# In the second attention, the softmax probabilities are multiplied by the inverse totals on GpSimd instead of VectorE

## What is computed

```
q = einsum('btd,ndh->btnh', x, q_kernel)             # 16 query heads of 128
k, v = einsum('bsd,ckdh->cbskh', x, kv_kernel)       # 8 key and value heads
q, k = rms_norm(q, q_scale), rms_norm(k, k_scale)
q, k = apply_rope(q, positions), apply_rope(k, positions)
mask = (j <= i) & (i - j < 128)
logits = einsum('btkgh,bskh->bkgts', q * 0.0884, k), masked
probs = softmax(logits, axis=-1)
enc = einsum('bkgts,bskh->btkgh', probs, v)
out = einsum('btnh,nhd->btd', enc, out_kernel)
```

## Time and profile before

| | us |
|---|---|
| median of 3 runs | 989.39 |
| lowest, highest | 989.05, 1001.19 |
| the profiled execution | 989.41 |
| its span | 987.8 |
| tiles 0 to 7 of attention b, in the span | about 403.7 to 713 |
| DVE busy in the span | 630.9 (64%) |
| POOL busy in the span | 431.9 (44%) |
| PE busy in the span | 779.2 (79%) |

### The profile page before, as it was taken

One profiled execution on the slowest core, in us unless ns is written; L12 is line 12 of the kernel. 1 busy time (PEld: TensorE's weight loads), 2 busy tenths in 40 slices (PEclk: granted clock), 3 DMA queues, 4 the chain that ended last, 5 costly groups with the idle time before them and its releaser, 6 DMA issues.

```text
span 987.8 us, 17657 instructions
## 1 busy us (share of the span) xinstructions
PE 779.2 (79%) x4548; PEld 663.9 (67%) x4548; DVE 630.9 (64%) x2152; ACT 505.6 (51%) x1274; POOL 431.9 (44%) x340
## 2 busy tenths in 40 slices
PE   5897837989898306789999999999878689988841
PEld 4465726888788204567887878788766688888830
DVE  3565624667667267689778788797465467776522
ACT  2332314667677322565565665556423477777621
POOL 2004773657666513123122132130647267667551
PEclk9997977999999659799999999999959799999955
DMA  9955736888798430000000000000234689889645
GB/s 351 426 208 198 259 125 187 210 203 224 195 228 186 91 107 1 1 1 1 1 1 1 2 1 1 1 17 1 107 118 142 196 217 229 215 217 227 147 90 167
DMA packets 65591, 130.85 MB, mean 132 GB/s; under 512 B 8388, under 2 KB 36420, under 8 KB 63872
## 3 DMA queue, kind: packets, MB, share of 16 engines
q1 hardware_dynamic: 41104, 93.77, 28.5%
q0 software_dynamic: 24432, 36.44, 17.6%
HBM read 75.25 MB, written 54.92 MB: 132 GB/s over the span
## 4 chain that ended last, share of the span: by engine, by line
PE 34%; DVE 18%; issue 15%; DMA 15%; POOL 8%; ACT 6%; SPq 1%; DVEq 1%; POOLq 1%; ACTq 1%
DMA raw<-in_w_gate_up 6%; PE bank L315 6%; POOL token_rows L1791 6%; PE bank L317 5%; PE bank L316 5%; DMA over<-token_rows 3%; PE bank L852 3%; PE bank L817 3%; DVE over L1670 2%; PE bank L841 2%; PE bank L650 2%; DVE halves L1498 2%; DVE over L1626 2%; DVE over L1632 2%; PE bank L558 2%
## 5 line engine op out<-in xcount | busy, mean ns | idle before, releaser
L315 PE MATMUL bank<-halves 88*128 88x256 f32 (+2 forms) x548 | 193.4, 353 | 32.0 <-DVE halves L1498 19.0
L317 PE MATMUL bank<-halves 88*128 88x256 f32 (+2 forms) x548 | 173.5, 317 | 0.0
L316 PE MATMUL bank<-halves 88*128 88x256 f32 (+2 forms) x548 | 173.3, 316 | 0.0
L315 PEld LDWEIGHTS bank<-halves 128*128 128x128 f32 (+1 forms) x548 | 108.8, 198 | 51.7 <-issue 41.1
L1791 POOL DMA_INDIRECT token_rows<-xn,slot_ids x96 | 98.8, 1030 | 101.8 <-issue 69.3
L316 PEld LDWEIGHTS bank<-halves 128*128 128x128 f32 (+1 forms) x548 | 109.9, 201 | 0.9
L317 PEld LDWEIGHTS bank<-halves 128*128 128x128 f32 (+1 forms) x548 | 108.6, 198 | 1.0
L1480 DVE TENSOR_TENSOR over<-over,bank 128x176 f32<-128x176 f32 x128 | 42.6, 333 | 72.8 <-ACT over L1026 72.3
L1893 POOL TENSOR_TENSOR over<-over 128x512 f32<-128x512 f32 x16 | 20.6, 1285 | 144.5 <-DVE over L1632 144.5
L1165 ACT ACTIVATE over<-over,nb,rqs 128x256 f32<-128x256 f32 (+1 forms) x128 | 71.7, 563 | 10.8 <-DVE nb L1658 10.8
L1002 ACT ACTIVATE halves<-raw 128x704 fp32r<-128x704 f32 x64 | 50.5, 790 | 50.5 <-DMA raw<-in_w_gate_up 47.1
(11 more groups left out here) (214 smaller groups left out, 2030.5 us busy)
## 6 DMA issues: line engine op xcount, KB each, us to landing
raw<-in_w_gate_up SPq DMA_DIRECT2D x64, 352.0 KB, 4.0
over<-token_rows SPq DMA_DIRECT2D x64, 320.0 KB, 3.4
token_rows<-over SPq DMA_DIRECT2D x10, 1536.0 KB, 21.1
raw<-in_w_down SPq DMA_DIRECT2D x64, 176.0 KB
over<-in_w_qkv_b SPq DMA_DIRECT2D x1, 4096.0 KB, 14.4
raw<-in_w_shared SPq DMA_DIRECT2D x6, 384.0 KB, 3.2
w_out_b_sb<-in_w_out_b SPq DMA_DIRECT2D x1, 2048.0 KB, 25.0
raw<-in_w_gate_up POOLq DMA_DIRECT2D x5, 352.0 KB, 4.4
```

Source lines behind the costliest of these rows:

```text
L315: nc.tensor.matmul(out, hi, rhs_lo, start=start, stop=False)
L316: nc.tensor.matmul(out, lo, rhs_hi, start=False, stop=False)
L317: return nc.tensor.matmul(out, hi, rhs_hi, start=False, stop=stop)
```

## The change

The two DVE multiplies of a group (L1670) become one POOL multiply over both heads, with the inverse totals broadcast. DVE keeps the reciprocal, which now counts up a semaphore `rl` of its own. POOL's order becomes: for each group of tile t the multiply of g, then, for g below 6, the rotation of chunk g of tile t+1 with all that hangs on it (for chunk 2 the wait for `rk` and the two L1900). The rotations of tile 0 come ahead of the loop as before. The two norm steps that stood around the multiply on DVE now follow the reciprocal.

```diff
-            def probabilities(t, g, newton):
+            def reciprocals(t, g):
                 n = NKV * t + g
-                keys = slice(0 if t % BT else P, 2 * P)
                 dve.wait_ge(bb["exp"], n + 1)
-                steps.did(nc.vector.reciprocal(rl[:, n % 4, :], lsum[:, n % 4, :]))
-                newton()
-                steps.wait()
-                for h in range(2):
-                    last = nc.vector.tensor_scalar(p_b[:, n % 2, h, keys], p_b[:, n % 2, h, keys],
-                                                   rl[:, n % 4, h:h + 1], None, ALU.mult)
-                last.then_inc(bb["p"], 1)
-                newton()
+                nc.vector.reciprocal(rl[:, n % 4, :], lsum[:, n % 4, :]).then_inc(bb["rl"], 1)
...
                 for g in range(NKV):
                     if g == 0 and more and (t + 1) % BT == 0:
                         rest_of_rows((t + 1) // BT)
-                    probabilities(t, g, norms.step)
+                    reciprocals(t, g)
+                    norms.step()
+                    norms.step()
...
+            def rotation(t, c):
+                n = KQ * t + c
+                pool.wait_ge(bb["rotated"], n + 1)
...
+                if c == K_CHUNKS:
+                    pool.wait_ge(bb["rk"], t + 1)
+                    pool.wait_ge(bb["rot"], n)
+                    for k in range(K_CHUNKS):
...
+            def probabilities(t, g):
+                n = NKV * t + g
+                first = 0 if t % BT else P
+                pool.wait_ge(bb["rl"], n + 1)
+                of = p_b[:, n % 2, :, first:2 * P]
+                scale = rl[:, n % 4, :].unsqueeze(2).to_broadcast([P, 2, 2 * P - first])
+                nc.gpsimd.tensor_tensor(of, of, scale, ALU.mult).then_inc(bb["p"], 1)
+
+            for c in range(KQ):
+                rotation(0, c)
             for t in range(TILES):
-                for c in range(KQ):
...
+                for g in range(NKV):
+                    probabilities(t, g)
+                    if t + 1 < TILES and g < KQ:
+                        rotation(t + 1, g)
             ffn_pool(pool, 1, sums_1)
```

More of the change, by code:

```diff
@@ L80 @@
 STEPS_LN = 2 * BT + STEPS_RSQRT
-STEPS_B = BATCHES * STEPS_LN + TILES * (2 * STEPS_RSQRT + 1) + 3 * NKV * TILES
+STEPS_B = BATCHES * STEPS_LN + TILES * (2 * STEPS_RSQRT + 1) + 2 * NKV * TILES
 RSQRT_MAGIC = float(0x5F3759DF)
@@ L251, in program @@
         bb = phase("b", "step xn xnT xhi xlo whi wlo tab proj sq rotated sum rk rot krot t_mm t v"
-                        " s_mm max exp p pt_mm pt e_mm e o_mm x")
+                        " s_mm max exp rl p pt_mm pt e_mm e o_mm x")
         block = ctx.enter_context(nc.Block())
@@ L1882, in _ @@
             KQ = K_CHUNKS + Q_CHUNKS
-            for t in range(TILES):
-                for c in range(KQ):
[L1885 to L1902, removed]
@@ new lines, in rotation @@
+            def rotation(t, c):
+                n = KQ * t + c
+                pool.wait_ge(bb["rotated"], n + 1)
+                if c >= 4:
+                    pool.wait_ge(bb["t_mm"], KQ * t + T_ORDER.index(c - 2) + 1)
+                elif t:
+                    last = c if c < K_CHUNKS else c + 2
+                    pool.wait_ge(bb["t_mm"], KQ * (t - 1) + T_ORDER.index(last) + 1)
+                nc.gpsimd.tensor_tensor(roped[PLACE[c]], by_twos(rope_a[:, c % 2]), by_twos(rope_b[:, c % 2]),
+                                        ALU.add).then_inc(bb["rot"], 1)
+                if c == K_CHUNKS:
+                    pool.wait_ge(bb["rk"], t + 1)
+                    pool.wait_ge(bb["rot"], n)
+                    for k in range(K_CHUNKS):
+                        scale = rk[:, t % 2, k * CH:(k + 1) * CH].rearrange("p (i h) -> p i h", i=2)
+                        nc.gpsimd.tensor_tensor(roped[k], roped[k],
+                                                scale.unsqueeze(3).to_broadcast([P, 2, CH // 2, HD]),
+                                                ALU.mult).then_inc(bb["krot"], 1)
```

## The result

The changed kernel takes 1028.52 us (median of 4 runs, 1023.89 to 1031.75), the kernel before 989.22 beside it (4 runs). The ratio is 1.040, with a 95% interval of 1.0356 to 1.0443: 39 us slower. The forecast was 1013 and its range ended at 1021. The profiled execution took 1023.89 us, with a span of 1022.3. In the new numbering the reciprocal is L1665, the copy of `rk` L1689, the rotation L1886, the scaling of the keys L1893 and the new multiply on POOL L1903.

A forecast was written before the change was run, and what follows sets the result against it. PE was taken to set the pace in full tiles, its waits for DVE's multiply worth at most 16.6 us. Group 3 stalls in tiles 0 to 6 plus 0.4 in tile 7 made 23.9 us on 989.41: 1013, range 1001 to 1021.

The forecast's parts named there:

- the price of the multiply: One POOL multiply of a group takes 1.04 us in a full tile and 0.62 in a half-size one.
- the give-backs of the sum: PE's existing group 4 wait before L829 disappears after the stall: 0.31 us in tile 2, 1.24 in 1, 1.90 in 0.
- The scatter: POOL's first-half token scatter starts 8.0 us later, just hidden by 0.9 us before the second half's; booked 0.
- The sum: Net group 3 stalls of tiles 0 to 6 plus 0.4 in tile 7: 23.9 us on 989.41, giving 1013.
- The terms: Group 3 stall per tile: end of `rk` plus 3.26 us (2.84 half-size) minus L829's former start; 4.81 in tile 2.
- DVE's lead: How much earlier DVE copies `rk`: 0 in tiles 2, 3 and 6, 0.3 us in the others; bounds 0 and 1.9.
- The ordinary groups: Groups 0, 1, 2 and 4 to 7: probabilities ready about 2.5 us after the rotate; nothing booked beyond group 3.
- The hold of DVE: POOL's multiply behind each rotation holds DVE's L265 in group 2 and L1658 in each group about 1 us longer.
- rival 1: L265 gets in when the rotation ends, so `rk` comes 0.75 to 0.9 us earlier per tile: 1008 us, chance 0.20.
- My counter-evidence: L1670 issued at 499.51 under the second L1900 seemed held through the next POOL instruction: 1.63 us instead of 0.62.
- Rivals 2 and 3: No hold matters and `rk` comes earlier: 1002 us, chance 0.10; relief of DVE ends PE's waits: 973 us, chance 0.03.
- Rival 4: Other groups also wait, a multiply costs 1.29 us, the scatter loses cover: 6 to 10 us more, about 1020, chance 0.17.

The follow-up runs named there:

- The order of the queue: Changed kernel with POOL's wait for `rk` and the two key scalings moved behind the multiply of group 3: 993.71 us, ratio 1.0047 to the kernel before.
- The filler: Changed kernel plus 16 matmuls of 512 columns, result overwritten, on PE ahead of its group 3 wait in tiles 0 to 6: 1015.07 us, ratio 1.0235.
- the idle multiply: Kernel before plus a POOL multiply into an unused buffer wherever the change puts one; DVE keeps its own: 1003.30 us, ratio 1.0165.
- both versions with late rotations: Changed kernel, key scalings behind group 3's multiply, four rotations behind the next group's: 987.02 us, 1.0034; same with POOL multiplying only in tiles 0, 1, 4, 5: 988.35, 1.0008.
- POOL's multiplies in four tiles: Changed kernel with key scalings and four rotations moved later, POOL multiplying only in tiles 0, 1, 4, 5, DVE elsewhere in old order: 988.35 us, ratio 1.0008.

## Why the prediction was wrong

**What held.** The change made the kernel slower; the loss lies in attention b, in group 3 of tiles 0 to 6, directly behind the key scalings; the price of the multiply was right; the probabilities no longer keep PE waiting in group 4, as the give-backs of the sum want; the first transposes of tile 7 waited 1.47 us instead of 1.00, 0.47 more where the sum has 0.4. The scatter was hidden, as booked: the second half's followed at 770.75 after a wait of 0.60 us, where POOL stood 8.99 us before. Its cover of 9 us is used up. The order of the queue was worth 35 of the 39 us.

**The step that failed.** The sum prices a stall by its own length and lets what lies behind it keep its length: "Everything behind attention b starts later by this and keeps its length", and no part of it says otherwise of the work inside attention b. The profile of before showed PE at 1.00 in full tiles and busy nearly without a gap, and I didn't ask what a gap of 4 us does to that. It dropped the granted clock to 0.50, during the stall or just behind it: from group 3 to group 4 the mean was 0.51, 0.68, 0.65, 0.74, 0.71, 0.69 and 0.74 in tiles 0 to 6. From the start of group 3 to the start of group 4, against the same stretch before without its wait, the seven tiles took 2.4, 2.07, 2.58, 1.7, 1.35, 1.96 and 1.7 us longer: 13.8 us together, the 14.3 of the stage by another count. The filler, which leaves the stall in its length and fills it, brought 16 us back, and its trace is 14.3 us shorter in the same seven stretches. 1013 and 14 is 1027; measured 1028.5. The Trainium skill has the pattern, in "TensorE: Matmul & The Clock Gate", section "HAM oscillation": a wait that recurs lets the engine fall to its lower level, and the work behind each wait starts cold. There the wait is for a DMA; the trace agrees for one on another engine's queue, with 0.50 in the 3.47 us behind it. The prediction used that skill for the port only.

**The sum of the waits was right by luck.** Errors cancelled in it. Group 3's transposes started later, counted from the first L829 of their tile, in tiles 0 to 6, by 2.99, 3.97, 4.14, 4.12, 3.28, 3.89 and 2.98 us: 25.4 in sum. The terms were 4.06, 4.75, 4.81, 4.81, 4.06, 4.75 and 3.1: 30.3. Most of the difference is DVE's lead. By the same count `rk` ended earlier by 1.28, 0.99, 0.58, 0.57, 0.99 and 1.07 us in tiles 0 to 5 and by nothing in tile 6: 5.5 in sum, where I had taken 1.2. The give-backs of group 4 were 5.7 us instead of 6.9. What made up for it is a wait that the sum doesn't have, at PE's transposes of chunks (L801, group 4, directly behind each stall), which wait for ACT's copies; before, then after:

```profile
PE bank L801 <- ACT over L1156: 1.8, 4, 0.8
```

```profile
PE bank L801 <- ACT over L1156: 5.1, 7, 1.4
```

It took 0.58 us in tiles 1, 2, 3, 5 and 6 and 1.36 and 0.80 in tiles 0 and 4. It stays with the filler, at a clock of 1.00 (5.4 us), and is 1.4 us where the order of the queue leaves no stall. So it comes with the stall and not with the clock. Of PE's 23.2 us of added idle time these are 3.3, and 20 are waits before L829. The ordinary groups, where I had booked nothing, added nothing: the waits before L829 outside groups 3 and 4 were 7.1 us before and 7.7 after, and 0.47 of the difference is tile 7.

**The hold of DVE.** L1658 was held as forecast. L265 wasn't held through the multiply that was queued behind the rotation: it got in between, as the Trainium skill has it in "SBUF — State Buffer", section "Who interferes with whom", and as rival 1 said. My counter-evidence was misread. Row 499.51 in the earlier trace rows is a pair in one row; taken apart, the trace of the kernel before has the first at 499.51 for 0.35 us and the second at 499.77 for 1.36 us. The second L1900 ends at 499.67 and the first multiply at 499.86: it got in between L1900 and the rotation behind it, and only the second was held by that rotation, which ends at 500.98. So each waited for one instruction of POOL, as in the idle multiply's pair. The prediction also tells of steps with both inputs in SBUF only; L265 and L267 read one tensor each, and were held all the same. Rival 1 had the lead of `rk` nearly right, but for tile 6; what it doesn't have is the hold of L267 behind L265. It had no clock either, so its 1008 is further off. Rivals 2 and 3 are out. Rival 4 has a wait behind the stall, and one came, at L801 and for ACT, 3.3 us instead of its 6 to 10 in all; its multiply price and its uncovered scatter didn't come.

## What to carry to other kernels

An operation moved to an idle engine is moved into a queue, and it inherits every wait that stands ahead of it there: read the order of the waits, not the busy share, and put the moved step ahead of the wait where its data allow (here 35 of 39 us). Where the receiving path is as long as the old one, relieving the loaded engine only changes the name of the wait. And when a change opens a gap of some microseconds in a TensorE stream that had none, price the work behind the gap too: here 1.4 to 2.6 us for each gap of 2.8 to 5.5 us.

## What was unexpected of the hardware

- A gap in PE of 3.90 us cost 2.5 us more by the clock behind it (7.46 instead of 4.94 us); idle matmuls of 4.01 us in the gap avoided it.
- Gaps of 1.88, 2.05 and 2.63 us left the clock at 1.00, and gaps of 2.52 and 2.69 us didn't. In tile 0 both versions with late rotations have waits of 2.49 us in group 3 and 2.30 us in group 4; the clock stayed at 1.00 in one and was 0.50 from 419.40 to 426.10 in the other (POOL's multiplies in four tiles).
- POOL's 128 x 512 multiply holds tiny steps of DVE too: 0.96 us for an int32 step (L267) on 128 x 8 that took 0.17 as L270 in the same tile, and 0.99 instead of 0.16 for L1658.
- A multiply on POOL that nobody waits for cost 1.65%; in tile 2 it and the rotation ahead of it held DVE's pair of multiplies for 1.14 us.
